# Attention key norms as two reduced-precision passes over squares that GpSimd splits, query norms first

## The reference

```
q, k, v = complex projections of x, 16 heads of 64 complex numbers
qr, kr  = q * phase(t), k * phase(t)
s  = real(qr . conj(kr))                       # per head, 512 x 512, causal
qn = sum(|q|^2),  kn = sum(|k|^2)              # over the 64 complex numbers
maha   = max(qn_i + E^2 kn_j - 2 E s_ij, 0) / V
logits = coef * log1p(maha / nu) - 32 log V    # E, V: of the distance i - j
out    = softmax(logits) v;  y = out @ Wo
```

## Time and profile before

| what | us |
| --- | --- |
| median of 3 runs | 1696.05 |
| lowest and highest | 1693.87, 1697.52 |
| span of the profiled execution | 1693.8 |
| PE busy | 1642.7 (97%) |
| DVE busy | 1483.9 (88%) |
| ACT busy | 1452.4 (86%) |
| POOL busy | 974.3 (58%) |
| POOL rotation L1495, 127 times | 303.2 busy, 470.0 idle before |
| PE key norms L1196, 127 times in two records | 131.2 |

### The profile page before, as it was taken

The page is one execution under the profiler, slowest core; times in us unless marked ns, Lnnn a source line. Parts: engine busy times, 40 slices in busy tenths (PEclk is TensorE's granted clock), DMA queues, the critical chain, the costliest instruction groups (busy, mean ns, idle before and its releaser), DMA issues. The chain is left out here.

```text
span 1693.8 us, 30993 instructions
## 1 busy us (share of the span) xinstructions
PE 1642.7 (97%) x9690; PEld 1337.0 (79%) x9690; DVE 1483.9 (88%) x3380; ACT 1452.4 (86%) x2909; POOL 974.3 (58%) x826
## 2 busy tenths in 40 slices
PE   5999988999999999999999999999999999899998
PEld 4787866888888888888788888888887887777876
DVE  6878877999899989999999998999899989977665
ACT  6677678999999999999999999999999999765765
POOL 3564546566566656665655565566566656345565
PEclk9999999999999999999999999999999999999999
DMA  6000032232223322232232323232332222100000
GB/s 177 1 1 1 1 103 66 63 91 62 77 70 75 74 68 79 63 78 65 77 79 63 91 57 82 54 91 60 82 79 63 69 70 51 26 7 7 13 11 15
DMA packets 50482, 100.03 MB, mean 59 GB/s; under 512 B 8208, under 2 KB 25872, under 8 KB 50320
## 3 DMA queue, kind: packets, MB, share of 16 engines
q1 hardware_dynamic: 50320, 98.07, 22.5%
HBM read 17.95 MB, written 5.24 MB: 14 GB/s over the span
## 5 line engine op out<-in xcount | busy, mean ns | idle before, releaser
L1495 POOL TENSOR_TENSOR early<-early 128x1024 f32<-128x1024 f32 x127 | 303.2, 2387 | 470.0 <-PE pS L1183 258.6
L654 POOL TENSOR_TENSOR hid_lo_d<-hid_d,hid_hi_d 128x512 fp32r<-128x512 f32 x176 | 231.5, 1316 | 218.7 <-ACT hid_hi_d L559 212.1
L1387 ACT ACTIVATE early<-early,qnorm 128x128 f32<-128x128 f32 (+3 forms) x512 | 247.0, 554 | 68.3 <-DVE early L1578 66.4
L1183 PE MATMUL pS<-early 128*128 128x128 f32 (+3 forms) x1024 | 297.6, 433 | 0.3 <-PEq L105 0.3
L1371 ACT ACTIVATE early<-early,nmax 128x128 f32<-128x128 f32 (+3 forms) x512 | 281.6, 562 | 6.9 <-DVE nmax L1565 6.7
L1183 PEld LDWEIGHTS pS<-early 128*128 128x128 f32 x1024 | 164.7, 191 | 96.0 <-issue 61.4
L1574 DVE SCALAR_TENSOR_TENSOR pS<-pS,ek 128x1280 f32<-128x1280 f32 x128 | 191.4, 1495 | 55.3 <-PE pS L1183 54.4
L1504 POOL TENSOR_TENSOR ek<-early 128x128 f32<-128x128 f32 (+3 forms) x256 | 216.7, 881 | 3.6 <-ACT early L1379 3.0
L1504 POOL TENSOR_TENSOR ek<-decay,early 128x128 f32<-128x128 f32 (+3 forms) x256 | 215.3, 876 | 0.0
L1400 ACT ACTIVATE early<-early,params 128x512 f32<-128x512 f32 (+1 forms) x256 | 196.9, 819 | 0.0
L1198 PEld LDWEIGHTS pV<-ones,early 128*128 128x128 f32 x1016 | 134.3, 193 | 61.3 <-issue 61.3
(11 more groups left out here) (394 smaller groups left out, 3883.7 us busy)
## 6 DMA issues: line engine op xcount, KB each, us to landing
early<-early SPq DMA_DIRECT2D x263, 256.0 KB, 3.6
early<-trig_d SPq DMA_DIRECT2D x64, 64.0 KB, 2.0
trig_d<-early SPq DMA_DIRECT2D x3, 1024.0 KB, 6.9
early<-in_w SPq DMA_DIRECT2D x3, 704.0 KB, 9.0
x_sb<-in_x SPq DMA_DIRECT2D x4, 512.0 KB, 8.4
early<-in_wqk SPq DMA_DIRECT2D x16, 128.0 KB, 3.4
cos<-trig_d SPq DMA_DIRECT2D x32, 64.0 KB, 2.3
sin<-trig_d SPq DMA_DIRECT2D x32, 64.0 KB, 2.1
```

The costliest lines, as they stand in the source:

```text
L654: g.tensor_tensor(hid_lo[:, par], hid[:, par], hid_hi[:, par].bitcast(F32), ALU.subtract).then_inc(lo_done, 1)
L1183: last = pe.matmul(s.pS[:, span(I)], rot[:, I * P:(I + 1) * P], rot[:, N:N + (I + 1) * P], start=True, stop=True)
L1387: last = a.activation(u[:, span(I)], u[:, span(I)], ACT.Relu, bias=qnorm[:, r % 2, I:I + 1])
L1495: g.tensor_tensor(rot[:], by_cos[:], crossed[:], ALU.add).then_inc(S["rot_done"], 1)
```

## The change

The key norm was one fp32 matmul of a matrix of ones over the keys' squares. It becomes two fp32r passes of the ones: over the high part of the squares (rounded to fp32r) and over the low part (the rest). POOL makes both parts, a copy and a subtraction of 128x512, at the head of its step, ahead of the rotation. PE takes the query norms first and then waits for the low part. The squares of the next pair wait for the key norms instead of the query norms. The two parts lie in the buffer of the low weights of the down product (`w2s[1]`), so these are written to DRAM after the weights are split and read back after the last key norm; the first down product of the last phase waits for that. Pair 0, whose norms the dense phase makes (line 440), stays as it was.

```diff
--- before.py
+++ after.py
@@ -249,6 +249,7 @@
 
                 sp.wait_ge(w13_lo, len(PIECES))
                 sp.wait_ge(w2_lo, len(PIECES2))
+                sp.dma_start(s.w2_lo_d, s.w2s[1][:, 0:2 * N].bitcast(F32)).then_inc(s.S["w2_lo_out"], 16)
                 sp.dma_start(wv_raw, s.wv.rearrange("h d k -> d h k")).then_inc(wvo_in, 16)
                 sp.dma_start(wo_raw, s.wo.rearrange("h d k -> d h k")).then_inc(wvo_in, 16)
                 sp.wait_ge(cst_in, 32)
@@ -343,6 +344,8 @@
                 c, k, par = e // HC, e % HC, e % 2
                 if first and c == 0:
                     pe.wait_ge(w2_lo, 1 + sum(k >= lo for lo, hi in PIECES2[1:]))
+                if last_phase and e == 0:
+                    pe.wait_ge(s.S["w2_lo_in"], 16)
                 pe.wait_ge(lo_done, e + 1)
                 if k == 0:
                     wait(pe, x_done, c - 1)
@@ -1049,6 +1052,7 @@
         wqk = (s.wqk0, [sb(f"wqk1_{half}", [P, 2 * P], F32R) for half in ("hi", "lo")])
         decay2, wqk_raw, by_cos, by_sin, crossed = s.decay2, s.wqk_raw, s.by_cos, s.by_sin, s.crossed
         squares, rot, knorm, u, z = s.squares, s.rot, s.knorm, s.u, s.z
+        key_hi, key_lo = s.key_sq
         qnorm = sb("qnorm", [P, 2, TILES])
         ek = sb("ek", [P, SW])
         probT = [sb(f"probT{k}", [P, SW]) for k in range(2)]
@@ -1170,6 +1174,9 @@
                     load_trig(building(TRIG, i, r))
                 if building(EXPAND, i, r):
                     expand(building(EXPAND, i, r))
+                if i * 16 + r == PAIRS - 1:
+                    sp.wait_ge(S["kn_done"], PAIRS)
+                    sp.dma_start(s.w2s[1][:, 0:2 * N].bitcast(F32), s.w2_lo_d).then_inc(S["w2_lo_in"], 16)
 
             steps(nc.sync, a_step)
 
@@ -1193,11 +1200,13 @@
                     pe.wait_ge(D["rstd_done"], 1)
                 if live(i, r - 2) and parity(r - 2) == 0:
                     wait(pe, S["val_done"], values_made(i, r - 2))
-                pe.matmul(s.p6[:], s.ones[:], squares[:, N:2 * N], start=True, stop=True).then_inc(S["kn_done"], 1)
                 for I in range(TILES):
                     last = pe.matmul(s.p5[:, I:I + 1], squares[:, I * P:(I + 1) * P], s.ones[:, 0:1],
                                      start=True, stop=True)
                 last.then_inc(S["q2_done"], 1)
+                wait(pe, S["key_lo"], n)
+                pe.matmul(s.p6[:], s.ones[:].bitcast(F32R), key_hi, start=True, stop=False)
+                pe.matmul(s.p6[:], s.ones[:].bitcast(F32R), key_lo, start=False, stop=True).then_inc(S["kn_done"], 1)
 
             def project(i, r):
                 n, par, b = i * 16 + r, parity(r), r % B
@@ -1402,7 +1411,7 @@
             def square(i, r):
                 n = i * 16 + r
                 wait(a, S["cos_done"], n + 1)
-                wait(a, S["q2_done"], n)
+                wait(a, S["kn_done"], n)
                 a.activation(squares[:], s.pQK[:], ACT.Square).then_inc(S["sq_done"], 1)
 
             def values_out(i, r):
@@ -1504,9 +1513,19 @@
                     last = g.tensor_tensor(ek[:, span(I)], decay[par][:, span(I)], knorm[:, 0:(I + 1) * P], ALU.mult)
                 last.then_inc(S["ek_done"], 1)
 
+            def split_squares(i, r):
+                n = i * 16 + r
+                if n == 1:
+                    g.wait_ge(S["w2_lo_out"], 16)
+                g.wait_ge(S["sq_done"], n + 1)
+                g.tensor_copy(key_hi, squares[:, N:2 * N]).then_inc(S["key_hi"], 1)
+                g.wait_ge(S["key_hi"], n)
+                g.tensor_tensor(key_lo, squares[:, N:2 * N], key_hi.bitcast(F32), ALU.subtract).then_inc(S["key_lo"], 1)
+
             def a_step(i, r):
                 if live(i, r + 1):
                     if (i, r) != (0, -1):
+                        split_squares(i, r + 1)
                         rotate(i, r + 1)
                     spread(i, r + 1)
                 if i == 0 and r == -1:
@@ -1780,11 +1799,13 @@
         ps = lambda name, shape: ctx.enter_context(nc.psum_tensor(name, shape, F32))
         s = Shared(args, out)
         s.trig_d = nc.dram_tensor("trig_d", [3, H, DH // 2, N], F32, kind="Internal").ap()
+        s.w2_lo_d = nc.dram_tensor("w2_lo_d", [P, 2 * N], F32, kind="Internal").ap()
         s.x_sb = sb("x_sb", [P, TT, D])
         s.xT = [sb(f"xT_{h}", [P, B * N], F32R) for h in ("hi", "lo")]
         s.mv = sb("mv", [P, TT, 2])
         s.w13 = [sb(f"w13_{h}", [P, 2 * HC * P], F32R) for h in ("hi", "lo")]
         s.w2s = [sb(f"w2_{h}", [P, HC * P], F32R) for h in ("hi", "lo")]
+        s.key_sq = tuple(s.w2s[1][:, k * N:(k + 1) * N] for k in range(2))
         s.wr = sb("wr", [P, 2 * NE], F32R)
         s.wp = [sb(f"wp_{h}", [P, H * P], F32R) for h in ("hi", "lo")]
         s.params = sb("params", [P, H, NPAR])
@@ -1817,7 +1838,8 @@
                  "lam_done qk_done bs_done crossed_in cos_done sq_done rot_done norm_done q2_done qn_done kn_done "
                  "ek_done s_done w_done t_done relu_done ln_done zred_done exp_done v_done "
                  "val_done tr_done trc_done av_done rinv_done acc_done stat_done dve_passed pool_passed sp_passed "
-                 "late_stat late_mv late_var late_ln late_root late_rstd late_step late_xn late_xt late_hi late_lo mv_done expanded0 expanded1")
+                 "late_stat late_mv late_var late_ln late_root late_rstd late_step late_xn late_xt late_hi late_lo mv_done expanded0 expanded1 "
+                 "w2_lo_out w2_lo_in key_lo key_hi")
         s.S = {n: ctx.enter_context(nc.semaphore(n)) for n in names.split()}
         names = ("guw_done silu_done var_done ln_done root_done rstd_done xn_dve xt_done xhi_done xlo_done "
                  "logit_done gap_done exp_done w_done wexp_first wb_done head_step")
```

## The result

The changed kernel takes 1729.62 us (median of four runs, 1728.12 to 1733.14) against 1696.78 for the kernel before: ratio 1.0194, 95% interval 1.0175 to 1.0213. It is slower by 1.9%. The forecast was 1749 with a range from 1702 to 1790.

What follows compares the result with a forecast made beforehand. PE, 97% busy, was taken as the bound, with ScalarE and VectorE close behind. New steps of about 9.84 us, 0.43 above the mean, over 124 give +53: 1694 + 53 = 1747, plus 2 to the median: 1749 us, range 1702 to 1790.

Steps and rivals of the forecast that it cites:

- value steps: Attention steps with value products, eight in a run: forecast 9.84 us against 10.04, -0.20, with no stall for the split.
- plain steps: Attention steps without value products, eight after each eight with them: forecast 9.82 us against 8.69, +1.13.
- 512 KB exchange: Low weights written out after 27 us, read back after the last key norm; no reader for 37 us, so free.
- The order as such: PE's query norms going first keep their price of 0.81 us; squares waiting on key norms instead cost nothing.
- no collision: Rival: GpSimd's copy doesn't hold VectorE or slips in ahead; plain step 9.1 us, total 1705 to 1712; chance 0.17.
- main case: Attention: both kinds of step about 9.84 us, VectorE and GpSimd getting in each other's way; 1735 to 1775 us, chance 0.61.
- GpSimd's busy time: Sign over the whole kernel: POOL busy near 1240 us if the forecast is right.
- last piece: VectorE's 256-column L1565 piece, 0.41 us in the loop; sign: stretched to near 1.2 us or the copy late behind it.
- ring of a plain step: Squares, copy, subtraction, key passes, projection, transposes and back to squares, through three engines: 9.82 us against 8.69.
- the row taken: L1488, a one-input POOL instruction of 128x512 at 0.78 us, used as the price of the copy.
- piece of minima still running: VectorE's L1565 piece before the last, still running when the copy wants to start: 0.3 us in the loop.
- regular steps of 9.84: Both kinds of attention step at about 9.84 us, 0.43 above the mean of 9.41, counted 124 times.

## Why the prediction was right, and where it was not

*Direction and rough size* were right: slower, value steps -0.18 us (forecast -0.20, 9.84 against 9.86 measured), plain steps the place of the loss, and the 512 KB exchange free (it is read back from 1488.70 us on, in 3.2 us, and PE's first down product of the last phase, at 1528.54, waits for no transfer). The order as such is free, as costed. But the size is less well met than the range suggests: +53 us were forecast and +33 measured, and 1729.6 lies in none of the forecast's cases, above the 1705 to 1712 of "no collision" and below the 1735 to 1775 of the main case. That it lies in the range is partly luck. Of the signs, GpSimd's busy time came out (1230 us, 1240 forecast), but PE waited 0.6 us instead of 1.2 to 1.6, the last piece took 0.89 us instead of about 1.2, and the granted clock fell in places, to a mean of 0.99.

*The step that failed* is the ring of a plain step, 9.82 us forecast, 9.11 measured. Three of its terms were off. The copy was sized at 0.78 and takes 0.61 us when nothing is in its way. That lies half way between the row taken and the 0.43 us estimated from the Trainium skill ("GPSIMD Engine Reference", section 4.1), so neither the row nor the "roughly line-rate" of the Trainium skill was the price. The piece of minima still running (0.3) and the last piece (0.41) were put into the split's loop: "Whichever goes first, the split loses about that piece". The split loses next to nothing: the copy starts 0.06 us behind the squares, the subtraction 0.08 us behind the copy and takes 1.32 us instead of the 1.27 of the kernel without a copy, and VectorE alone is held. Without these and with the copy's own 0.61 the sum is 8.94, in line with the 8.9 above, and below the measured step.

*And the loop is not what bounds the step.* The forecast treated VectorE as near the bound but with room, and read its hold as a delay of the split. It left out VectorE's own queue, 8.70 us long in a plain step, as a second path. The runs show the reverse: plain step = 8.70 (VectorE's own queue, shown by the passes without the split) + the time its last piece is held (0.41, 0.34 or 1.09 in three kernels). The rival "no collision" named 9.1 us and so nearly the measured step, but its total of 1705 to 1712 is as far off as the forecast, and its mechanism is the opposite one: its 9.1 was the loop without the collision, and the collision is what costs.

*What the sum left out.* The 63 plain steps at +0.41 are 26 us. The first plain step went from 8.62 to 9.81 in five of the eight runs of plain steps, 4 us beyond the 0.41 (its third piece meets the copy and its fourth the subtraction), and six steps of 11.0 to 16.8 us took 23 us more than at the same places before, 20 beyond the 0.41. That makes 50, more than the 44.6 measured, since steps that were disturbed before (9.2 to 9.7 us) absorb some of it. So the loss has another make-up than forecast: in place of an even +1.13 stand +0.41 and a few very long steps. The forecast also set its regular steps of 9.84 against a mean of 9.41 that holds the disturbed ones; against the regular 10.04 and 8.69, mean 9.37, it would have come out 5 us higher. One of the very long steps, changed kernel, VectorE and GpSimd:

```profile
655.86 1.06 DVE L1584 CUSTOM_DVE_ANT_0 early<-early,params 128x384 f32<-128x384 f32 x1
...
655.90 0.61 POOL L1521 CAST w_lo<-early 128x512 fp32r<-128x512 f32 x1 [1.39 <-ACT early L1415]
...
656.59 1.46 POOL L1523 TENSOR_TENSOR w_lo<-early,w_lo 128x512 fp32r<-128x512 f32 x1
...
656.85 1.75 DVE L1584 CUSTOM_DVE_ANT_0 early<-early,params 128x512 f32<-128x512 f32 x1
...
658.12 2.74 POOL L1504 TENSOR_TENSOR early<-early 128x1024 f32<-128x1024 f32 x1
...
658.53 2.61 DVE L1584 CUSTOM_DVE_ANT_0 early<-early,params 128x256 f32<-128x256 f32 x1
```

VectorE came to its four minima at 655.58 here, 0.3 us ahead of the copy instead of 1.5. In the first plain step of each eight that is the rule, since the copy comes early in it. But here the second piece, issued 0.04 us ahead of the copy, was held too (1.06 instead of 0.61 us); in a first plain step of 9.80 it is issued 0.10 ahead and takes 0.62. So the third piece met the subtraction (1.75 instead of 0.75) and the fourth the rotation (2.61 instead of 0.48).

Each held piece ends 0.28 to 0.55 us behind the GpSimd instruction that held it (the third at 658.60, the subtraction at 658.05), 0.20 us less than the piece takes undisturbed, while the next GpSimd instruction is the longer for it (2.74 instead of 2.40 for the rotation). So a waiting piece is let in between two GpSimd instructions, but only one, and the piece behind it meets the next. The whole step shifted by one partner, and the longest partner is the rotation. PE then stood idle for 3.25 us and its granted clock fell too (0.87 of full in this step), which lengthens it further. In the run with the rotation after the minima this step is 9.80, but there its pieces already met as in the regular first steps. What the rotation's wait does is seen better in the piece of 2.87 us above, which takes 0.74 with it.

## What to carry to other kernels

Before work is moved to an engine that has room, ask which instructions of the other engines share something with it, and line up the new instructions with them in time: here 0.4 us of overlap with an engine that had no slack outweighed the gain. A bound must be shown by removing it: taking PE's 0.38 us away changed nothing in plain steps, and taking 0.7 us of GpSimd work away made the kernel slower. Where steps differ in their bound, apply a change only to the steps in which its cover exists; that turned +1.9% into -0.5%. Where a chain of short instructions meets a chain on another engine, a start that shifts by less than 0.1 us can pair each with a longer partner.

## What was not expected of the hardware

A copy on GpSimd takes 0.61 us alone (128x512, f32 to fp32r), but 0.97 when it is issued while a piece of minima runs (534.85 above, in the run with the key squares first). The piece ends at 535.35 and the copy 0.47 us later, so most of the copy seems to have come after the piece; VectorE's next piece is then held in its turn.

TensorE's granted clock fell behind some of the new waits. In the changed kernel, around 523 us, behind an idle time of 1.05 us (PE in order of time, then the window):

```profile
523.46 0.50 PE L1208 MATMUL pV<-w_lo,ones 128*128 128x512 f32 x1 [1.05 <-POOL w_lo L1523]
...
524.56 0.63 PE L72 MATMUL pQK<-xT_lo,wqk_hi 128*128 128x512 f32 x1
...
524.99 0.63 PE L73 MATMUL pQK<-xT_hi,wqk_hi 128*128 128x512 f32 x1
...
525.41 0.63 PE L71 MATMUL pQK<-xT_hi,wqk_lo 128*128 128x512 f32 x1
```

```profile
524.50:527.50 3.00, 3.00 (x11) 2.35 (x10) 2.52 (x6) 2.46 (x5) 3.00 (x4) 0.53 0.04 15
```

The granted clock of the window is 0.53 of full speed, so mostly the lower of the two levels, 1.2 instead of 2.4 GHz, and passes start 0.43 us apart instead of 0.25. The step took 11.03 us; with the rotation after the minima the same step has a wait of 1.00 us (519.32 above), a clock at full, and takes 9.50. The same happened in 26 of the 63 plain steps of the run with the split after the minima (idle times of 1.1 us, steps of 11.1 instead of 9.54, mean clock 0.969), and hardly at all where PE waited 0.6 us or less. Not every wait of 1.1 us was followed by it: most other plain steps of that run have it too and keep the full clock. What decides stays open.
